# The last layer of a four-layer transformer: half of its normalisation and one quantisation step on ScalarE, and a value bias inside the product

## The reference, cut to what matters

```
V = (v @ wv.T + bv).reshape(b, -1, H, DK).transpose(0, 2, 1, 3)          # layer 2; layer 3 alike
...
def _L3_ffn_ref(x, weight_int8, weight_scale, bias):
    x2 = x.reshape(-1, K)
    x_scale = jnp.maximum(jnp.abs(x2).max() / 127.0, EPS)
    x_int8 = jnp.clip(jnp.round(x2 / x_scale), -128, 127).astype(jnp.int8)
    acc_i32 = jax.lax.dot_general(x_int8, weight_int8.T, ...)
    out = acc_i32.astype(jnp.float32) * x_scale * weight_scale.T
    out = out + bias
...
x = x + _L3_ffn_ref(_layernorm(x, axis=-1), L3_ffn_weight_int8, L3_ffn_weight_scale, L3_ffn_bias)
```

## Time and profile before

| what | value |
|---|---|
| median of 3 runs | 1589.87 us (1588.41 to 1591.91) |
| the profiled execution | 1589.54 us |
| its span from the first to the last instruction | 1587.7 us |
| mean granted TensorE clock | 0.832 |
| busy: TensorE, VectorE, ScalarE, GpSimd | 1205.8, 1010.5, 612.6, 256.2 us |
| instructions | 22618 |

### The profile page before, as it was taken

One profiled execution on the slowest core, in us unless ns is written; L12 is line 12 of the kernel. 1 busy time (PEld: TensorE's weight loads), 2 busy tenths in 40 slices (PEclk: granted clock), 3 DMA queues, 4 the chain that ended last, 5 costly groups with the idle time before them and its releaser, 6 DMA issues. The chain is left out here.

```text
span 1587.7 us, 22618 instructions
## 1 busy us (share of the span) xinstructions
PE 1205.8 (76%) x6805; PEld 878.8 (55%) x6805; DVE 1010.5 (64%) x3444; ACT 612.6 (39%) x1154; POOL 256.2 (16%) x240
## 2 busy tenths in 40 slices
PE   4788799999866652235926886999999999758862
PEld 2656589899744452113614554677777777425531
DVE  7778746666648859833357775565556665446768
ACT  3475434444332231011224651444444444336631
POOL 1334001001001000071474320000000000023401
PEclk9899889999965555566955996999999999769985
DMA  7342100000000040312224310000000000024301
GB/s 232 104 122 67 29 1 1 2 0 0 1 1 1 0 161 15 106 46 82 79 77 111 105 50 1 1 1 1 1 1 0 0 1 1 1 67 125 97 7 53
DMA packets 54757, 69.43 MB, mean 44 GB/s; under 512 B 6784, under 2 KB 35712, under 8 KB 54016
## 3 DMA queue, kind: packets, MB, share of 16 engines
q1 hardware_dynamic: 51328, 61.78, 13.5%
q0 software_dynamic: 3328, 6.43, 1.3%
HBM read 44.99 MB, written 23.59 MB: 43 GB/s over the span
## 5 line engine op out<-in xcount | busy, mean ns | idle before, releaser
L781 POOL TENSOR_TENSOR mha_ks<-KS,w_ctx 104x1024 fp32r<-104x1024 f32 (+1 forms) x48 | 90.9, 1895 | 681.8 <-POOLq L100 497.5
L2275 DVE SCALAR_TENSOR_TENSOR tree_hl<-tree_pH,tree_hh 128x512 fp32r<-128x512 f32 x192 | 132.4, 690 | 94.9 <-ACT tree_hh L2172 93.0
L2172 ACT ACTIVATE tree_hh<-tree_pH 128x512 fp32r<-128x512 f32 x192 | 114.6, 597 | 146.2 <-PE tree_pH L2076 146.2
L833 DVE TENSOR_REDUCE mha_nm<-mha_pS 128x16 f32<-128x1024 f32 x96 | 117.2, 1221 | 22.7 <-PE mha_pS L603 19.7
L1423 ACT ACTIVATE ffn_hid<-ffn_pH,w_ffn 128x512 f32<-128x512 f32 x128 | 85.5, 688 | 55.2 <-PE ffn_pH L1346 54.6
L2089 PE MATMUL tree_pY<-tree_hh,w2h 128*128 128x512 f32 x192 | 100.9, 525 | 4.8 <-DVE tree_hl L2275 4.7
L724 ACT ACTIVATE XH<-mha_pST 128x1024 f32<-128x1024 f32 x96 | 97.8, 1019 | 11.6 <-PE mha_pST L624 11.0
L603 PE MATMUL mha_pS<-mha_ks,mha_qs 96*128 96x256 f32 (+1 forms) x384 | 80.5, 337 | 25.8 <-DVE mha_nm L833 16.7
L1535 DVE SCALAR_TENSOR_TENSOR ffn_acc<-ffn_pE,ffn_wt,ffn_acc 128x128 f32<-128x128 f32 x192 | 54.0, 345 | 68.9 <-PE ffn_pE L1359 68.9
L1359 PEld LDWEIGHTS ffn_pE<-W2R,ffn_hid 128*128 128x128 f32 x768 | 94.6, 194 | 4.4 <-issue 0.2
L1359 PE MATMUL ffn_pE<-W2R,ffn_hid 128*128 128x128 f32 x768 | 95.2, 278 | 0.0
(11 more groups left out here) (476 smaller groups left out, 2779.0 us busy)
## 6 DMA issues: line engine op xcount, KB each, us to landing
mha_qs<-queries SPq DMA_DIRECT2D x72, 256.0 KB, 4.2
queries<-mha_qh SPq DMA_DIRECT2D x24, 256.0 KB, 2.1
queries<-mha_ql SPq DMA_DIRECT2D x24, 256.0 KB, 2.4
EW<-in_L_W_dram SPq DMA_DIRECT2D x32, 128.0 KB, 2.7
EW<-in_tree_full_dram SPq DMA_DIRECT2D x2, 1536.0 KB, 8.2
slots_in<-route_zero SPq DMA_DIRECT2D x4, 640.0 KB, 11.5
X<-in_x_dram SPq DMA_DIRECT2D x8, 256.0 KB, 7.2
exp_xe<-slots_in SPq DMA_DIRECT2D x16, 128.0 KB, 2.1
```

What stands on the lines that cost most here:

```text
L781: pool.tensor_tensor(ks[b % KB][0:K1, :, :, :], kb, hb, ALU.mult).then_inc(s["k"], 1)
L833: dve.tensor_reduce(nm[:, t, :], pS[:], AX.X, ALU.max, negate=True).then_inc(s["nm"], 1)
L2172: act.activation(hh[k % 2][:], pH[k % 2][:], ACT.Relu).then_inc(s["h"], 1)
L2275: dve.scalar_tensor_tensor(hl[k % 2][:], pH[k % 2][:], 0.0, hh[k % 2][:], ALU.max, ALU.subtract).then_inc(s["lo"], 1)
```

## The change

Three things change. In the layers 2 and 3 each of the 16 value products is begun by a product of one row (a row of ones by the row `bv`), so that PSUM holds the biased value; VectorE's 32 additions give way to plain copies, all eight of them on ScalarE in layer 2 (`on_act=4`), four on ScalarE and four on VectorE in layer 3. The row of ones is loaded with the context's constants, which widens that load by 128 columns. In the last layer ScalarE normalises the third and fourth tile of the groups 0 to 6, from `NB`, the negative mean times `rs`, which VectorE works out at the start; GpSimd and VectorE's reduction wait for it (`an`). ScalarE also takes the first of the three quantising operations (`scaled`), two groups ahead, and VectorE's finals are interleaved with its quantising, three groups behind.

```diff
         for b in range(B):
-            pe.matmul(pv[b // 4][:, P * (b % 4):P * (b % 4) + P], c2[:, b, :, :], w("wv"), start=True, stop=True).then_inc(s_v, 1)
+            to = pv[b // 4][:, P * (b % 4):P * (b % 4) + P]
+            if not key_mask:
+                pe.matmul(to, core.w("ctx", "one")[0:1, :], w("bv")[0:1, :], start=True, stop=False)
+            pe.matmul(to, c2[:, b, :, :], w("wv"), start=key_mask, stop=True).then_inc(s_v, 1)
...
-        if key_mask:
-            for n in range(2):
+        if not key_mask:
+            act.wait_ge(s_z, 2)
+        for n in range(on_act):
...
-        dve.wait_ge(s_z, 2)
-        bv = w("bv").rearrange("p (c h d) -> p c h d", h=2, d=HD)
-        for h in range(2):
-            q = slice(64 * h, 64 * h + 64)
-            dve.memset(VB[q, :, :, 2 * HD + h:2 * HD + h + 1], 1.0)
-            for n in range(4):
-                dve.wait_ge(s_v, 4 * n + 4)
-                src = values_of(pv[n], q, h)
-                dst = VB[q, 4 * n:4 * n + 4, :, h * HD:h * HD + HD]
-                for bb in range(4):
-                    dve.tensor_tensor(dst[:, bb], src[:, bb], bv[q, :, h, :], ALU.add)
+        if not key_mask:
+            dve.wait_ge(s_z, 2)
+            for h in range(2):
+                dve.memset(VB[64 * h:64 * h + 64, :, :, 2 * HD + h:2 * HD + h + 1], 1.0)
+        for n in range(on_act, 4):
+            dve.wait_ge(s_v, 4 * n + 4)
+            for h in range(2):
+                q = slice(64 * h, 64 * h + 64)
+                dve.tensor_copy(VB[q, 4 * n:4 * n + 4, :, h * HD:h * HD + HD], values_of(pv[n], q, h))
...
-        prep = prep_parts(core, 2, False, st, [pX[0][:], pX[1][:]], [pL[:], pM[:], pP[:], pR[:]])
+        prep = prep_parts(core, 2, False, st, [pX[0][:], pX[1][:]], [pL[:], pM[:], pP[:], pR[:]], on_act=4)
...
-            rs_act(act)
             act.activation(W8[:], core.W8i[:].bitcast(I8), ACT.Copy).then_inc(s["w8"], 1)
             act.activation(idb[:], ident, ACT.Copy).then_inc(s["w8"], 1)
+            act.wait_ge(s["nb"], 1)
+            for g in range(NG - 1):
+                for j in (2, 3):
+                    t = GT * g + j
+                    ins = act.activation(XH[:, t, :], X[:, t, :], ACT.Identity, bias=NB[:, t:t + 1], scale=RS[:, t:t + 1])
+                ins.then_inc(s["an"], 1)
+            rs_act(act)
+
+            def scaled(g):
+                x4 = XH[:, GT * g:GT * g + GT, :]
+                act.activation(x4, x4, ACT.Identity, bias=magic[:], scale=xs[:, 0:1]).then_inc(s["q1"], 1)
+
+            act.wait_ge(s["inv"], 1)
+            scaled(0)
+            scaled(1)
             for g in range(NG):
+                if g + 2 < NG:
+                    scaled(g + 2)
                 act.wait_ge(s["qTp"], g + 1)
...
                 pool.wait_ge(s["b"], g + 1)
+                pool.wait_ge(s["an"], min(g + 1, NG - 1))
...
+            dve.memset(magic[:], MAGIC)
+            dve.scalar_tensor_tensor(NB[:, READY], MV[:, READY, 0], -1.0, RS[:, READY], ALU.mult, ALU.mult).then_inc(s["nb"], 1)
             for g in range(NG):
                 if g == NG - 1:
                     rs_dve(dve)
-                for j in range(GT):
+                for j in range(GT if g == NG - 1 else 2):
...
                 dve.wait_ge(s["b"], g + 1)
+                dve.wait_ge(s["an"], min(g + 1, NG - 1))
...
-                link(dve.tensor_scalar(x4, x4, xs[:, 0:1], MAGIC, ALU.mult, ALU.add))
+                dve.wait_ge(s["q1"], g + 1)
...
+            for g in range(NG):
+                quantise(g)
+                if g >= 3:
+                    final(g - 3)
+            for g in range(NG - 3, NG):
+                final(g)
...
-    out["ctx"] = [("ident", np.eye(P, dtype=np.float32)),
+    out["ctx"] = [("one", np.ones((1, P), np.float32)), ("ident", np.eye(P, dtype=np.float32)),
```

More of the change, by code:

```diff
@@ L167, in values_of, with prep_parts @@
     return bank[q, :].rearrange("p (b c h d) -> p b c h d", b=4, h=2, d=HD)[:, :, :, h, :]
-def prep_parts(core, L, key_mask, st, pk, pv, between=None):
+def prep_parts(core, L, key_mask, st, pk, pv, between=None, on_act=2):
     KS, VB = core.KS[L], core.VB[L]
@@ L221, in on_vector @@
                     between(dve, NQ * n + g)
-        if key_mask:
-            for n in range(2, 4):
-                dve.wait_ge(s_v, 4 * n + 4)
-                for h in range(2):
-                    q = slice(64 * h, 64 * h + 64)
-                    dve.tensor_copy(VB[q, 4 * n:4 * n + 4, :, h * HD:h * HD + HD], values_of(pv[n], q, h))
-            return
-        dve.wait_ge(s_z, 2)
-        bv = w("bv").rearrange("p (c h d) -> p c h d", h=2, d=HD)
-        for h in range(2):
-            q = slice(64 * h, 64 * h + 64)
-            dve.memset(VB[q, :, :, 2 * HD + h:2 * HD + h + 1], 1.0)
-            for n in range(4):
-                dve.wait_ge(s_v, 4 * n + 4)
-                src = values_of(pv[n], q, h)
-                dst = VB[q, 4 * n:4 * n + 4, :, h * HD:h * HD + HD]
-                for bb in range(4):
-                    dve.tensor_tensor(dst[:, bb], src[:, bb], bv[q, :, h, :], ALU.add)
+        if not key_mask:
[7 more added lines that the diff above has]
+                dve.tensor_copy(VB[q, 4 * n:4 * n + 4, :, h * HD:h * HD + HD], values_of(pv[n], q, h))
     return on_tensor, on_scalar, on_vector
@@ L2346, in quantised_linear @@
         qT, yo = two("qT", [P, GT_P], BF16), two("yo", [P, GT, P])
+        NB, magic = st.sb("NB", [P, T]), st.sb("magic", [P, 1])
         am, amr, one, xs = st.sb("am", [P, NG]), st.sb("amr", [P, P]), st.sb("one", [1, P]), st.sb("xs", [P, 2])
@@ L2350, in quantised_linear @@
         pY = [st.ps(f"pY{u}", [P, 512]) for u in range(2)]
-        names = "w8 own amx amt am1 xsp xq qTp qT Y o b out".split()
+        names = "w8 own amx amt am1 xsp xq qTp qT Y o b out nb an inv q1".split()
         s = {n: st.sem(n) for n in names}
@@ L2420, in _, with quantise, final @@
             link(dve.tensor_scalar(xs[:, 1:2], pB[:, 0:1], 1.0 / 127.0, EPS, ALU.mult, ALU.max))
-            link(dve.reciprocal(xs[:, 0:1], xs[:, 1:2]))
-            for g in range(NG):
+            dve.reciprocal(xs[:, 0:1], xs[:, 1:2]).then_inc(s["inv"], 1)
+            def quantise(g):
                 x4 = XH[:, GT * g:GT * g + GT, :]
-                link(dve.tensor_scalar(x4, x4, xs[:, 0:1], MAGIC, ALU.mult, ALU.add))
+                dve.wait_ge(s["q1"], g + 1)
                 link(dve.tensor_scalar(x4, x4, MAGIC, 127.0, ALU.subtract, ALU.min))
                 dve.tensor_scalar(XQ[:, GT * g:GT * g + GT, :], x4, -128.0, None, ALU.max).then_inc(s["xq"], 1)
-            for g in range(NG):
+            def final(g):
                 dve.wait_ge(s["Y"], g + 1)
```

## The result

The changed kernel took 1596.12 us (median of 7 runs, 1591.90 to 1599.53) against 1589.63 of the kernel before (7 runs, 1586.60 to 1591.91). The ratio is 1.0054 with a 95% interval of 1.0037 to 1.0070: about 8.6 us slower by the ratio (the two medians lie 6.5 apart), where 8.2 faster was forecast. The profiled execution has a span of 1593.7, 6.0 longer than before.

The account below looks back on a forecast made before the run. VectorE was taken to set the last 43 us; routing waited on TensorE's late signals beside GpSimd's scatters. From 1589.54, -2.8 - 2.7 - 4.2 + 1.2 + 0.3 = -8.2 gave 1581.3 us, range 1577 to 1587.5.

Parts of the forecast that it names:

- Layer 3's preparation, +1.2: Layer 3's values: 32 added one-row passes at 0.117 each, copies replacing VectorE's additions; stage ends 1.2 us later.
- Rival E: Layers 2 and 3: bias passes dear, TensorE held in routing; 1593.3 at 0.26 a pass, 1594.9 at 0.29; chance 0.08.
- Routing stage, -4.2: Layer 2: VectorE's additions go, added passes lie beside GpSimd's scatters, mask checks follow earlier; 4.2 us shorter.
- Rival B: Layer 2's routing: scatters hold TensorE itself, not its signals; stage worth +0.3, total 1585.8; chance 0.24.
- First part, -2.8: Last layer's normalisation: two of four tiles leave VectorE, period 2.19 to 1.68, GpSimd starts 0.3 later; 2.8 us shorter.
- Second part, -2.7: Last layer's quantising and finals: ScalarE takes the first step, one stall of 0.58; 19.1 instead of 21.78 us.
- Rival D: Last layer's quantising: ScalarE sets the pace, 0.80 a group instead of 0.52, 2.2 lost; total 1586.2; chance 0.08.
- Load, +0.3: Loading the constants: 64 KB more on 1092 KB that took 5.1 us costs 0.3 us.

Follow-up runs that it names:

- 128 rows: Changed kernel with each bias product over 128 rows (a matrix of 1/128) instead of one row, same passes and order: 1580.20 against 1587.12, ratio 0.9967.
- regrouped: Changed kernel with all 16 one-row bias products ahead of the 16 value products, which start anew, so values lack their bias: 1582.61 us, one run.
- no bias: Changed kernel without the bias products in layers 2 and 3, copies as in the change: 1573.68 against 1587.12, ratio 0.9908.
- wide products: Changed kernel with one one-row bias product of 512 columns per bank, four in all, ahead of the values: 1584.30 against 1587.98, ratio 0.9973.

## Why the prediction was wrong, step by step

**The step that failed is "Layer 3's preparation, +1.2"**, and in it the choice that a one-row pass costs what a value pass costs (0.117), as "nearest in width and in what surrounds it". Measured: +14.5. The working priced the added passes by a pass among its like, put the change from one kind to the other at nothing, and left the value passes at 0.117. In fact each change costs about 0.19, and with one after every second pass both kinds slow down: 64 passes x 0.208 = 13.3 against 32 x 0.117 = 3.7, which is +9.6 at the full clock (31 changes x 0.19 and 64 x 0.112 make 13.1). The rest of the 20.6 that the passes took, 7.3, is the clock, which the alternating passes did not keep up; the copies give 2.4 back. The runs separate the three candidates: alternation of equal rows costs nothing (128 rows: 0.112), a one-row pass costs nothing extra by itself (regrouped: 0.12), and only the mixture does.

The Trainium skill has a sentence that may bear on this and was not weighed: "TensorEngine Tiling (Array Packing)", Tiling Modes, says that changing the tiling mode, the rows and columns of the tile in use, drains TensorE. It has no price for it and does not say that a product of one row is another mode. The traces agree as far as they go: in the regrouped run the slow steps at the full clock stand at a change (0.20) and right behind it (0.21), and nowhere else. Another page of the Trainium skill, "TensorE: Matmul & The Clock Gate", Why this matters for your kernels, has a product of 32 rows take the time of one of 128; for one row the regrouped run agrees (0.12, beside 0.117 for the value passes of the kernel before).

The price stood in the trace of the kernel before, in other rows of the line that the earlier trace rows quote. Those in the earlier trace rows ran at 1.2 GHz (granted clock 0.50), which the prediction does not say; the same six-row line ran at 2.4 GHz elsewhere, between products of 128 rows:

```profile
230.12 0.39 PE L1363 MATMUL ffn_pA<-w_ffn,ffn_hid 128*128 128x128 f32 x2
230.44 1.15 PE L1335 MATMUL ffn_pI<-b2R,ffn_wT 6*128 6x128 f32 x8
231.52 0.50 PE L1344 MATMUL ffn_pH<-ffn_xTh,up_h 128*128 128x512 f32 x1
```

```profile
199.80:201.60 1.80, 1.80 (x8) 1.76 (x8) 0.00 (x0) 0.00 (x0) 0.00 (x0) 0.50 0.00 0
230.40:231.60 1.20, 1.20 (x10) 1.05 (x9) 0.69 (x1) 0.00 (x0) 0.00 (x0) 1.00 0.00 0
```

Two passes of 128 rows ahead of the change take 0.32 (230.12 to 230.44) where two among their like take 0.22, and the eight of six rows 1.08 (to 231.52) where eight of 0.112 take 0.90. Start by start it is 0.20 to 0.21 at either change and right behind the first, and 0.112 between them: the price of the regrouped run. Not every difference in rows costs this: in the same trace products of 107 rows follow products of 99 rows near 82.2, and the starts at that change stay 0.12 apart. Which property of a product makes a change dear was not tried.

Rival E came near in size: at 0.29 a bias pass it gave 1594.9. That is luck, since its mechanism, dear bias passes, was not the one found, and its 0.26 and 0.29 are rows at half the clock. Worked back, the 16.9 that the passes grew by are 0.53 for each bias pass, more than any row that was set as a bound, because the neighbours and the clock are in them too.

**"Routing stage, -4.2"** failed in its sentence that the additional passes lie ahead of 719 beside the scatters; it was worth -1.1. Rival B named this, TensorE itself being held, but not its size: it had some 40 passes left at 719, and the run has 11. The condition was missed: with 32 or 40 passes it is not held and the step gives its 4.3 (no bias, wide products); with 64 it is held behind the 40th to 47th, and what is left has to run after the scatters. What holds it is open. It is not the number of signals. That instructions reach TensorE slowly while GpSimd issues indirect transfers would fit both the gaps put down to "issue" and the count of passes, but no run here shows it; without the scatters the stage was not tried. The trace speaks against code being loaded as the reason: from 690 to 725 of the changed kernel all 704 packets of its DMA queues were the scatters', and none was of the queues that carry instructions. Nor can the rows tell whether the late signals of the first passes are late signals or early records.

**"First part, -2.8"** measured -2.9: the period is 1.68 and GpSimd starts when ScalarE's second tile ends, as worked out. **"Second part, -2.7"** measured -2.7: start 0.89 after the reciprocal (0.86), one stall of 0.51 (0.58), 2.18 a group (2.2). Rival D, ScalarE's pace, did not come; with the step back on VectorE the part is 2.7 longer. The rule of the Trainium skill that the prediction quoted ("ScalarE: Activation LUTs", Rules for kernel authors), additions and multiplications on VectorE and not on ScalarE, is right on the single operation here (0.80 to 0.82 for ScalarE's scaling, where the estimate from that page had 0.80, beside VectorE's 0.48) and did not decide, since VectorE was the engine that was waited for.

**"Load, +0.3"** cannot be told from the spread of the stages ahead of the scatters; the load itself landed in 5.3 instead of 5.1.

## What to carry to other kernels

A cheap product with few rows put between products of 128 rows is paid at both changes, in its own passes and in its neighbours', and by the clock; make the bias product as tall as the rest, or as wide as a bank and in a gap in which TensorE waits for others. Price an insertion by the run of instructions that it interrupts and not by its own row: look in the trace for a place where the two kinds already meet, and read the starts there, at the granted clock of the place where the new product will stand. An engine that seems idle beside another engine's DMA issues may have room only for a limited number of instructions, here 40 to 47 passes.

## What had not been expected of the hardware

- One-row passes between 128-row passes: 0.208 each at 2.4 GHz and 0.36 at 1.2 GHz, for both kinds; 0.112 to 0.117 for each kind among its like. A single change from one row to 128 costs two slow steps, 0.20 and 0.21 at 2.4 GHz.
- The clock fell from 1.00 to 0.50 while TensorE was busy without a gap with such passes (from 1389.80 to about 1393.2), and fell also behind one-row passes among their like; with 128 rows, in the same place and number, it stayed at 1.00.
- Beside GpSimd's indirect transfers TensorE ran 40 to 47 passes without a gap and then one every 0.7 to 2.8, with 16 signals and with 4.
